# 118 spare 128x128 products on TensorE ahead of batch 0's steps, in a two-layer attention, expert and state-space kernel

## The chip, the cores and the metric

The kernel runs on one core of one Trainium2 chip. A core has TensorE (products and transposes, results into PSUM banks), VectorE, ScalarE and GpSimd for everything else, and queues that issue DMAs; SyncE's queue issues all of this kernel's. The engines run side by side, each through its own list of instructions in order, and wait for one another by semaphores. The metric is the time on the device of one execution, in microseconds, the median of several runs; lower is better.

## The reference

The input `x` is 4 batches of 512 rows of 128 features, with a context of 77 rows of 96 features for each batch. Four residual layers follow one another, each on a LayerNorm of `x`:

```python
x = x + L0_xattn(layernorm(x), ctx, ctx, ...)      # 16 heads of 8 features, 77 keys, softmax
x = x + L0_ffn(layernorm(x), ...)                  # 8 experts 128 -> 512 -> 128, the top 2 weighted
x = x + L1_xattn(layernorm(x), ctx, masks, ...)    # top-32 attention of 4 heads, FiLM, a state-space
                                                   # convolution by Fourier transform, a GELU MLP
x = x + L1_ffn(layernorm(x), rhs)                  # one product in int8 values with scales
```

All expert products are computed for all rows, in float32; the two picked experts get a weight and the others zero. The convolution's kernel is generated from its parameters inside the program (the `kgen` steps).

## The kernel before, in words

Everything is held on chip: rows on the 128 partitions, four tiles of 128 rows to a batch. The program is a list of 690 steps `(kind, batch, index)`. Five streams of steps, head and attention (H), experts (E), text attention (T), tail (O) and kernel generation (K), are merged into one list, `order`, by a string written out by hand (`ORDER`, line 138, read by `plan`). Each engine's block loops over that same list and does its part of each step, so the list sets the order of work on every engine. TensorE's block is the loop at line 632.

PSUM has eight banks here: two for the experts' first product (`moe_h`), two for their second (`moe_y`), four (`side`) that all other steps take in turn; a step's product waits until the former contents of its `side` bank were read. `moe_h[0]` is first written by the first expert product of batch 0.

Batch 0's steps up to the first expert product come in this order. A small setup of keys and values (lines 633 to 653). `norm_T` attn: four 128x128 transposes of the normalised input (line 629). `q_proj` (line 672), whose result ScalarE and VectorE split in three bf16 pieces that twelve DMAs spread over partitions (line 594). Four `setup_film` products (line 658), which wait for weights that GpSimd scales (line 1481), then `setup_rhs`. `smax`: 32 small bf16 products (line 681), whose row maxima VectorE takes (line 1100); `smax_T`: their transposes (line 629 again), which four DMAs spread (line 601). `kgen_base`: 43 short VectorE instructions (lines 1306 to 1348). Then the sixteen heads: `score` h (line 696, bf16, 50 rows by 77 columns of weights), an exponential on ScalarE (line 923), and `pv` h (line 706, float32, 77 by 72), one head behind. Two buffers `PT` take the exponentials.

Between scores 9 and 10 stands `kgen_tables` 0: VectorE's tables (lines 1360 to 1372), ScalarE's sines and exponentials (lines 980 to 988), GpSimd's products (lines 1516 to 1524). Behind them on ScalarE stands `attn_sum` 0 (line 927), which empties the bank of heads 0 to 7, after a reciprocal on VectorE (line 1110). `kgen_mm` 0 (line 852) stands before `pv` 15, and further tables before `attn_sum` 1. `attn_norm` (line 714), `o_proj` (line 721), LayerNorm, `norm_T` moe (line 629), `router` (line 727), the routing weights on VectorE (to line 1145), `w_T` (line 734), `b2_add` (line 741), and the first expert product `moe_up` (line 752). `moe_down` is line 764. Batch 1's head steps are then mixed with batch 0's experts.

A product of float32 operands leaves two MATMUL and two LDWEIGHTS records in the trace, a bf16 product or a transpose one each.

Of the kernel before, what the change touches and what calls it, by code (L numbers as in the profile page):

```python
# [14 lines left out]
P = 128  # L15
# [3 lines left out]
H0, HD0 = 16, 8  # L19
# [128 lines left out]
def needed(step, former):  # L148
# [10 lines left out]
    if kind == "score":  # L159
        return [("smax_T", b, 0)] + ([("pv", b, i - NPT)] if i >= NPT else [])  # L160
    if kind == "pv":
# [34 lines left out]
def plan():  # L196
# [9 lines left out]
    for run in ORDER.split():  # L206
        name = run[0]
        for _ in range(int(run[1:] or 1)):
# [11 lines left out]
         "score": 1, "attn_norm": 1, "o_proj": 1, "router": 1, "w_T": 1, "b2_add": 1, "text_q": 1, "topk": 1, "am_T": 1, "film": 1,  # L220
         "dft": 2, "idft": 1, "ffn_up": HC, "ffn_down": 1, "quant_T": 1, "quant_mm": 1, "kgen_mm": 1, "kgen_dft": 2}
SIDE = 4
NPT = 2


def place_fills(order):

    count, held, at, where = [0] * SIDE, set(), 0, {}

    def take(key):  # L230
        nonlocal at
        while at % SIDE in held:
            at += 1
        bank = at % SIDE
        where[key] = (bank, count[bank])
# [38 lines left out]
def recurrent_layers(nc, x, w1, w2, wpack, vpack, cpack, rpack, gpack, r2pack, xpack, dftf, dfti, b2, tmask, vmask, out):  # L274
# [10 lines left out]
    with ExitStack() as ctx:  # L285
        def sb(name, shape, dt=F32):
            return ctx.enter_context(nc.sbuf_tensor(name, shape, dt))

        def sem(name):
            return ctx.enter_context(nc.semaphore(name))  # L290
# [37 lines left out]
        def wc(name):  # L328
            return W[:, wcol[name][0]:wcol[name][1]]
# [16 lines left out]
        def xc(name):  # L346
            return XC[:, xcol[name][0]:xcol[name][1]]
# [29 lines left out]
        ZR = [m2.rearrange("p a s -> p (a s)").bitcast(F32), xnT["attn"]]  # L377
        PT = sb("PT", [NK, NPT, S])
        OV = qs
# [88 lines left out]
        moe_h = [ctx.enter_context(nc.psum_tensor(f"moe_h{i}", [P, 512], F32)) for i in range(2)]  # L468
        moe_y = [ctx.enter_context(nc.psum_tensor(f"moe_y{i}", [P, 512], F32)) for i in range(2)]
        side = [ctx.enter_context(nc.psum_tensor(f"side{i}", [P, 512], F32)) for i in range(SIDE)]  # L470


        side_full = [sem(f"side_full{i}") for i in range(SIDE)]
        side_read = [sem(f"side_read{i}") for i in range(SIDE)]
        x_in = [sem(f"x_in{b}") for b in range(B)]
# [39 lines left out]
        def free_for(pe, kind, b, i, n=0):  # L515

            k, m = FILL[(kind, b, i, n)]
            if m > 0:
                pe.wait_ge(side_read[k], m)
            return side[k], side_full[k]  # L520
# [7 lines left out]
        def emptied(eng, kind, b, i, n=0):  # L528

            k, m = FILL[(kind, b, i, n)]  # L530
            eng.wait_ge(side_read[k], m + 1)
# [14 lines left out]
        def pv_used(eng, b, h):  # L546

            if h % HG == HG - 1:
                k, m = FILL[("pv", b, 0, h // HG)]
                eng.wait_ge(side_full[k], m + 1)  # L550
            else:
                eng.wait_ge(pv_done, b * (H0 - 2) + h + 1 - h // HG)
# [70 lines left out]
        def _(pe):  # L623
# [6 lines left out]
                mm.then_inc(full, 1)  # L630

            for kind, b, i in order:
                if kind == "setup_k":
                    pe.wait_ge(xc_in, 16)
                    for n, w in enumerate(("wk", "wk1")):
                        dst, full = free_for(pe, kind, b, i, n)
                        pe.matmul(dst[:, 0:B * NK], xc(w), xc("ctxT"), start=True, stop=True).then_inc(full, 1)
                if kind == "setup_v":
                    dst, full = free_for(pe, kind, b, i, 0)
                    for b_ in range(B):  # L640
                        mm = pe.matmul(dst[0:NK, b_ * P:(b_ + 1) * P], xc("ctxT")[:, b_ * NK:(b_ + 1) * NK], xc("wv"),
                                       start=True, stop=True)
# [47 lines left out]
                if kind == "score":  # L690
                    dst, full = free_for(pe, kind, b, i)
                    if i == 0:
# [4 lines left out]
                              start=True, stop=True).then_inc(full, 1)  # L697
                if kind == "pv":

                    g, h = i // HG, i % HG  # L700
                    dst = side[FILL[("pv", b, 0, g)][0]]
                    if h == 0:
                        free_for(pe, "pv", b, 0, g)
                        pe.wait_ge(v_placed, b + 1)
                    emptied(pe, "score", b, i)
                    mm = pe.matmul(dst[0:GROWS, :], VP[:, g, GROWS * h:GROWS * (h + 1)], PT[:, i % NPT, :],  # L706
                                   start=(h == 0), stop=(h == HG - 1))
                    mm.then_inc(side_full[FILL[("pv", b, 0, g)][0]] if h == HG - 1 else pv_done, 1)
                if kind == "attn_norm":

                    dst, full = free_for(pe, kind, b, i)
                    for g in range(2):
                        pe.wait_ge(rz_ready, 2 * b + g + 1)
                        mm = pe.matmul(dst[64 * g:64 * g + 64, :], cc("spread")[64:GROWS, :], ZR[g][64:GROWS, :],
                                       start=True, stop=True)
# [7 lines left out]
                if kind == "router":  # L723
                    dst, full = free_for(pe, kind, b, i)
                    emptied(pe, "norm_T", b, "moe")
                    for t in range(T):
                        mm = pe.matmul(dst[:, t * E8:(t + 1) * E8], xnT_moe[:, b % 2, t * P:(t + 1) * P], wc("wr"),
                                       start=True, stop=True)
# [14 lines left out]
                if kind == "moe_up":  # L743
# [6 lines left out]
                    if n >= 2:  # L750
                        pe.wait_ge(moe_h_ready, n - 1)
                    pe.matmul(moe_h[n % 2][:], W1[:, e, c * P:(c + 1) * P], xnT_moe[:, b % 2, :],  # L752
                              start=True, stop=True).then_inc(moe_h_full, 1)
# [18 lines left out]
                if kind == "topk" and i[1] == 0:  # L772
                    t = i[0]
                    dst, full = free_for(pe, kind, b, t)
                    if t == 0:
# [5 lines left out]
                              start=False, stop=True).then_inc(full, 1)  # L781
# [26 lines left out]
                if kind == "idft":  # L808
# [3 lines left out]
                    for half in range(2):  # L812
                        for r in range(4):
                            y = (YR if r < 2 else YI)[:, r % 2, :, :]
                            mm = pe.matmul(dst[:, half * 2 * D:(half + 1) * 2 * D], FI[:, r, half * P:(half + 1) * P], y,  # L815
                                           start=(r == 0), stop=(r == 3))
# [40 lines left out]
        def _(act):  # L857
            for kind, b, i in order:
# [57 lines left out]
                if kind == "score":  # L916
                    src, read = filled(act, kind, b, i)
                    n = b * H0 + i
                    if i >= NPT:
                        pv_used(act, b, i - NPT)  # L920
                    elif b >= 1:
                        pv_used(act, b - 1, H0 - NPT + i)
                    act.activation(PT[:, i % NPT, :], src[0:NK, :], ACT.Exp).then_inc(read, 1)  # L923
# [674 lines left out]
```

## Time and profile before

| what | value |
|---|---|
| median of 3 runs | 673.56 us (670.68 to 678.76) |
| the profiled execution | 674.6 us, span 672.8 us |
| TensorE products busy | 526.3 us, 78% of the span, 2539 records |
| TensorE weight loads | 313.1 us, 47% |
| VectorE busy | 448.9 us, 67% |
| ScalarE, GpSimd busy | 239.6 us (36%), 136.6 us (20%) |
| mean granted TensorE clock | 0.844 |
| chain that ended last | TensorE 65%, VectorE 15%, issue 5% |

How to read it: the span is from the first to the last instruction of one profiled execution, and the device time includes a little around it. A busy share is an average over stages with different limits. The granted clock is the share of 2.4 GHz that TensorE is given: it is either 0.5 (1.2 GHz) or 1 (2.4 GHz), and a figure in between is a mean over a stretch.

### The profile page before, as it was taken

To read this page: it belongs to the slowest core of one execution; us is meant where nothing else is said; L and a number is where in the kernel's file an instruction comes from. 1 tells how busy PE (TensorE), PEld (TensorE's weight loads), DVE (VectorE), ACT (ScalarE), POOL (GpSimd) and SP (SyncE) were. 2 spreads that over 40 slices of the span, in tenths; PEclk is the share of its full clock that TensorE was granted. 3 is DMA by queue.
4 is the path that set the end of the run, shared out by engine and by line. 5 is a ranking of instruction groups with operands and counts; after the bars stand their busy time and mean duration, and the time that the engine had idled before them with its cause. 6 is when DMAs were issued, how large, how long until landed. Compare 5 with 4: busy or idle time off the path is not lost.

```text
span 672.8 us, 8058 instructions
## 1 busy us (share of the span) xinstructions
PE 526.3 (78%) x2539; PEld 313.1 (47%) x2539; DVE 448.9 (67%) x1770; ACT 239.6 (36%) x406; POOL 136.6 (20%) x164
## 2 busy tenths in 40 slices
PE   3449694297999999999999799999999974725360
PEld 2111133155644766644677665367657753403230
DVE  6279263638142458867577699678889978895616
ACT  3332541445434344344344264434354420411020
POOL 3501417232300020000142011015101151121211
PEclk8655555578999999999999899999999996755675
DMA  4519000003000003000002000000000000000000
GB/s 127 117 57 305 0 0 1 0 11 38 3 0 1 0 1 48 3 0 1 0 2 40 7 3 1 0 1 16 1 2 1 0 17 0 2 0 16 0 0 16
DMA packets 16156, 14.18 MB, mean 21 GB/s; under 512 B 1290, under 2 KB 14354, under 8 KB 16114
## 3 DMA queue, kind: packets, MB, share of 16 engines
q1 hardware_dynamic: 16114, 13.68, 8.5%
q8 instruction: 20, 0.33, 0.2%
q14 instruction: 22, 0.18, 0.1%
HBM read 8.86 MB, written 1.05 MB: 15 GB/s over the span
## 4 chain that ended last, share of the span: by engine, by line
PE 65%; DVE 15%; issue 5%; ACT 4%; SPq 4%; DMA 4%; POOL 2%; POOLq 0%; DVEq 0%
PE moe_y L764 15%; PE moe_h L752 15%; PE side L706 11%; SPq L594 4%; DMA QA<-Q 4%; PE side L696 4%; PE side L804 3%; PE side L815 2%; PE side L823 2%; PE side L792 2%; PE side L831 2%; DVE area L1184 2%; PE side L629 1%; PE side L852 1%; DVE TOP L1174 1%
## 5 line engine op out<-in xcount | busy, mean ns | idle before, releaser
L764 PEld LDWEIGHTS moe_y<-W,HT 128*128 128x128 f32 x1024 | 131.8, 194 | 45.6 <-issue 42.9
L764 PE MATMUL moe_y<-W,HT 128*128 128x128 f32 x1024 | 136.4, 279 | 0.0
L752 PE MATMUL moe_h<-xnT_moe,W 128*128 128x512 f32 x256 | 133.0, 608 | 0.0
L941 ACT ACTIVATE HT<-moe_h,W 128x512 f32<-128x512 f32 x128 | 87.6, 686 | 125.2 <-PE moe_h L752 124.7
L706 PE MATMUL side<-PT,VP 77*72 77x512 f32 x128 | 82.5, 735 | 0.7 <-ACT PT L923 0.7
L923 ACT ACTIVATE PT<-side 77x512 f32<-77x512 f32 x64 | 37.5, 591 | 59.6 <-PE side L696 59.5
L1160 DVE SCALAR_TENSOR_TENSOR X<-moe_y,RW,X 128x128 f32<-128x128 f32 x128 | 35.9, 343 | 25.1 <-PE moe_y L764 24.9
L752 PEld LDWEIGHTS moe_h<-xnT_moe,W 128*128 128x128 f32 x256 | 41.0, 195 | 13.0 <-issue 8.3
L1445 POOL TENSOR_TENSOR area<-area 128x128 f32<-128x128 f32 x16 | 7.3, 455 | 178.9 <-ACT area L958 178.9
L1184 DVE MATCH_REPLACE8 area<-TOP,area 128x77 f32<-128x77 f32 x192 | 40.6, 222 | 0.0
L696 PEld LDWEIGHTS side<-QA,KA 50*77 50x77 bf16 x64 | 7.1, 116 | 66.8 <-issue 59.0
L1100 DVE TENSOR_REDUCE mx<-side 128x6 f32<-128x462 f32 (+1 forms) x48 | 24.6, 577 | 20.1 <-PE side L681 20.1
L696 PE MATMUL side<-QA,KA 50*77 50x512 bf16 x64 | 28.4, 465 | 11.9 <-issue 6.3
L815 PE MATMUL side<-area,FI 128*128 128x256 f32 x64 | 19.2, 466 | 15.7 <-DVE area L1243 14.3
L1174 DVE MAX8 TOP<-area 128x8 f32<-128x77 f32 x192 | 31.2, 224 | 0.1
L681 PE MATMUL side<-KM,QA 128*128 128x154 bf16 x128 | 15.2, 266 | 13.7 <-DMA QA<-Q 13.3
L1110 DVE RECIPROCAL xT_head<-side 8x512 f32<-8x512 f32 x4 | 13.4, 3355 | 18.6 <-PE side L706 18.6
L792 PE MATMUL side<-FF,AMT 78*128 78x512 f32 x32 | 19.8, 705 | 6.9 <-ACT AMT L952 6.4
L706 PEld LDWEIGHTS side<-PT,VP 77*72 77x72 f32 x128 | 15.5, 160 | 20.1 <-issue 18.3
L815 PEld LDWEIGHTS side<-area,FI 128*128 128x128 f32 x64 | 15.0, 240 | 19.3 <-issue 16.4
L949 ACT ACTIVATE area<-area 128x308 f32<-128x308 f32 x16 | 7.4, 460 | 45.5 <-DVE area L1177 45.4
L785 PE MATMUL side<-C,AM 128*78 128x128 f32 x16 | 4.9, 307 | 22.1 <-DVE AM L1213 22.1
(306 smaller groups left out, 846.6 us busy)
## 6 DMA issues: line engine op xcount, KB each, us to landing
W<-in_w SPq DMA_DIRECT2D x8, 512.0 KB, 7.4
QA<-Q SPq DMA_DIRECT2D x48, 64.0 KB
X<-in_x SPq DMA_DIRECT2D x4, 256.0 KB, 6.2
out_dram<-FO SPq DMA_DIRECT2D x4, 256.0 KB, 2.3
V<-in_vpack SPq DMA_DIRECT2D x1, 579.0 KB, 3.5
area<-in_r2pack SPq DMA_DIRECT2D x1, 576.0 KB, 7.1
area<-in_gpack SPq DMA_DIRECT2D x1, 576.0 KB, 4.5
FW<-in_dftf SPq DMA_DIRECT2D x1, 512.0 KB, 7.5
```

Of the source, the lines that this page charges most:

```text
L594: sp.dma_start(QA[r0:r0 + HD0, :, :], Q3[64 * u:64 * u + 64, piece, :]).then_inc(q_spread, 16)
L696: pe.matmul(dst[0:NK, :], KA[r0:r0 + SROWS, i // 2, b * NK:(b + 1) * NK], QA[r0:r0 + SROWS, i // 2, :], start=True, stop=True).then_inc(fu ...
L706: mm = pe.matmul(dst[0:GROWS, :], VP[:, g, GROWS * h:GROWS * (h + 1)], PT[:, i % NPT, :], start=(h == 0), stop=(h == HG - 1))
L752: pe.matmul(moe_h[n % 2][:], W1[:, e, c * P:(c + 1) * P], xnT_moe[:, b % 2, :], start=True, stop=True).then_inc(moe_h_full, 1)
L764: mm = pe.matmul(moe_y[m % 2][:, t * P:(t + 1) * P], HT[:, m % 2, c, t * P:(t + 1) * P], W2[:, e, c, :], start=(c == 0), stop=(c == HC - 1))
L792: pe.matmul(dst[:], AMT[:, i % 2, :], FF[:, b, :], start=True, stop=True).then_inc(full, 1)
L815: mm = pe.matmul(dst[:, half * 2 * D:(half + 1) * 2 * D], FI[:, r, half * P:(half + 1) * P], y, start=(r == 0), stop=(r == 3))
L923: act.activation(PT[:, i % NPT, :], src[0:NK, :], ACT.Exp).then_inc(read, 1)
L941: act.activation(HT[:, m % 2, c, :], moe_h[n % 2][:], ACT.Relu, bias=wc("b1")[:, e * HC + c:e * HC + c + 1]).then_inc(moe_h_ready, 1)
L1160: ins = dve.scalar_tensor_tensor(X[:, b, t, :], moe_y[m % 2][:, t * P:(t + 1) * P], RW[:, b % 2, t, e:e + 1], X[:, b, t, :], ALU.mult, ALU ...
L1174: dve.max(TOP[:, a, h, r, :], s).then_inc(top_max, 1)
L1184: dve.match_replace(TW[:, h, :], TOP[:, a, h, r, :], s, PICKED)\
```

## The change

`SPARE` gives, for steps of batch 0, a number of spare products. TensorE issues them ahead of the step's own waits and work. Each multiplies two 128x128 blocks of weights that are in SBUF by then (`wq` and `wo`) into the first 128 columns of `moe_h[0]`, and nobody reads the result. They carry no wait and no signal. Counted by the list of steps there are 118: 16 + 12 + 8 + 6 + 12 + 4 + 3 + 20 + 4 + 16 + 3, and one for each of scores 2 to 15.

```diff
+SPARE = {("norm_T", "attn"): 16, ("setup_film", 0): 12, ("smax", 0): 8, ("smax_T", 0): 6, ("score", 0): 12,
+         ("attn_norm", 0): 4, ("o_proj", 0): 3, ("norm_T", "moe"): 20, ("router", 0): 4, ("w_T", 0): 16, ("b2_add", 0): 3,
+         **{("score", h): 1 for h in range(2, H0)}}
 NPT = 2
@@
             for kind, b, i in order:
+                for _ in range(SPARE.get((kind, i), 0) if b == 0 else 0):
+                    pe.matmul(moe_h[0][:, 0:P], wc("wq"), wc("wo"), start=True, stop=True)
                 if kind == "setup_k":
```

## Rows read from the trace of the kernel before

**Rows 1.** The page: busy tenths in 40 slices, TensorE and its granted clock.
```profile
PE   3449694297999999999999799999999974725360
PEclk8655555578999999999999899999999996755675
```
**Rows 2.** Stages: start:end, length, busy us (records) by engine, granted clock, DMA share, GB/s.
```profile
29.00:35.70 6.70, 3.00 (x20) 1.44 (x19) 0.81 (x2) 2.10 (x5) 1.65 (x6) 1.00 0.36 42
...
47.60:69.70 22.10, 21.32 (x27) 4.10 (x28) 19.08 (x37) 5.91 (x11) 3.29 (x2) 0.50 0.85 273
...
187.00:195.00 8.00, 8.00 (x19) 1.87 (x18) 2.15 (x5) 3.55 (x6) 0.00 (x0) 1.00 0.00 0
```
**Rows 3.** TensorE in order of time, to score 0: start, length, instruction [idle before].
```profile
15.87 1.09 PE L629 MATMUL side<-C,xn_head 128*128 128x128 f32 x4 [4.53 <-DVE xn_head L1077]
17.73 2.04 PE L672 MATMUL side<-xT_head,W 128*128 128x512 f32 x2 [0.78 <-ACT xT_head L897]
25.54 5.25 PE L658 MATMUL side<-area,VT 128*77 128x512 f32 x8 [5.77 <-POOL area L1481]
...
34.48 0.92 PE L681 MATMUL side<-KM,QA 128*128 128x154 bf16 x11 [3.51 <-DMA QA<-Q]
...
41.04 1.01 PE L629 MATMUL side<-C,mx 128*16 128x128 f32 x4 [1.51 <-DVE mx L1100]
47.63 0.65 PE L696 MATMUL side<-QA,KA 50*77 50x512 bf16 x2 [5.58 <-issue]
```
**Rows 4.** The same, heads of batch 0: a head, the next one's score, score 10.
```profile
50.91 0.65 PE L696 MATMUL side<-QA,KA 50*77 50x512 bf16 x1
51.48 1.98 PE L706 MATMUL side<-PT,VP 77*72 77x512 f32 x2
53.39 0.65 PE L696 MATMUL side<-QA,KA 50*77 50x512 bf16 x1
...
76.41 0.65 PE L696 MATMUL side<-QA,KA 50*77 50x512 bf16 x1 [5.54 <-ACT qs L927]
```
**Rows 5.** The same, two scores of batch 1.
```profile
188.41 0.41 PE L696 MATMUL side<-QA,KA 50*77 50x512 bf16 x1
...
189.76 0.41 PE L696 MATMUL side<-QA,KA 50*77 50x512 bf16 x1
```
**Rows 6.** The same, four 128x128 products cold and warm, warm steps, a short idle.
```profile
143.50 1.12 PE L764 MATMUL moe_y<-W,HT 128*128 128x128 f32 x8
144.46 0.60 PE L629 MATMUL side<-C,xn_head 128*128 128x128 f32 x4
145.84 1.10 PE L672 MATMUL side<-xT_head,W 128*128 128x512 f32 x2 [0.78 <-ACT xT_head L897]
...
162.69 2.00 PE L764 MATMUL moe_y<-W,HT 128*128 128x128 f32 x8
164.48 1.19 PE L681 MATMUL side<-KM,QA 128*128 128x154 bf16 x9
...
266.79 0.72 PE L681 MATMUL side<-KM,QA 128*128 128x154 bf16 x8 [1.60 <-DMA QA<-Q]
```
**Rows 7.** In order of time: table inputs on VectorE and ScalarE, then TensorE's late steps.
```profile
65.65 1.23 DVE L1372 TENSOR_TENSOR area<-area 128x1024 f32<-128x1024 f32 x1
...
71.95 1.04 ACT L984 ACTIVATE area<-area 128x1024 f32<-128x1024 f32 x1
...
75.79 0.57 ACT L927 ACTIVATE qs<-side 64x512 f32<-64x512 f32 x1
...
118.33 1.09 PE L629 MATMUL side<-C,xn_head 128*128 128x128 f32 x4 [4.89 <-DVE xn_head L1077]
...
126.28 1.06 ACT L984 ACTIVATE area<-area 128x1024 f32<-128x1024 f32 x1 [3.41 <-DVE area L1372]
...
132.75 1.01 PE L734 MATMUL side<-C,RW 128*8 128x128 f32 x4 [10.70 <-DVE RW L1145]
134.48 2.04 PE L741 MATMUL side<-B,xT_head 8*128 8x128 f32 x8 [0.72 <-issue]
```

## The prediction

> **What bounds the kernel now.** I read the page's slices first, then stages, then TensorE's own order in time. The slices [rows 1] are 16.8 us each: TensorE is above 90% from the twelfth slice to the thirty-third, so a microsecond lost or won before the first expert product stays in the end time nearly whole. The same rows show a granted clock of 0.5 in slices three to eight, about 34 to 135 us, which is exactly batch 0's attention. The stages [rows 2] say something less obvious: from 47.60 to 69.70 us TensorE is busy 21.32 of 22.10 us, and the clock is still 0.50 (the 1.2 GHz level) throughout. The same work in batch 1, 187 to 195 us, runs at 1.00 (2.4 GHz), with TensorE just as full. So this loop does not wake the clock by itself, but doesn't lose it once it has it. Its products are narrow: 50 of 128 rows for a score, 77 rows by 72 columns for a value product [rows 4]. What stood ahead of the rise at 29 us were the film products, 128 rows by 77 columns [rows 2, 3].
>
> Price of the low clock: one head (score start to score start) takes 53.39 - 50.91 = 2.48 us cold [rows 4] and 189.76 - 188.41 = 1.35 us warm [rows 5].
>
> The order of time [rows 3] gives the holes in front of TensorE's steps: 4.53 us before the first transposes, 5.77 before film, 3.51 before the maxima's scores, 1.51 before the maxima's transposes, 5.58 before score 0, and 5.54 before score 10 [rows 4]. The clock's memory shows too: after 3.51 us of idle at a high clock (30.97 to 34.48) the heads' stretch is cold [rows 2, 3], while after 1.60 us of idle up to 266.79 [rows 6] it was not lost: the slice around it, the sixteenth, has a granted clock of 9 tenths or more [rows 1].
>
> **The change, part by part.** It removes nothing, moves nothing, adds no wait and no DMA. It adds 118 products, 236 matmul records (a float32 product leaves two), each between two 128x128 operands. Their price: four such products from 162.69 to the next start at 164.48, so 1.79 / 4 = 0.45 us cold; from 143.50 to 144.46, so 0.96 / 4 = 0.24 us warm [rows 6]. They wait for nothing, so each starts as soon as the product ahead is through, and what matters is whether it ends before the step behind it was due.
>
> 1. Sixteen before the first transposes. TensorE is free at 15.87 - 4.53 = 11.34, the step starts at 15.87 [rows 3]. All warm: 3.8 us, hidden. All cold: 7.2 us, 2.7 late. I take half each, 5.5 us, 1.0 late, and then the transposes at 0.60 in place of 1.09 and the query product at 1.10 in place of 2.04 [rows 3, 6], which gives 1.4 back. Term -0.4, ends -1.4 and +2.7. The query's DMAs follow, so this moves everything behind it.
> 2. Twelve before film, eight before the maxima's scores: 5.4 and 3.6 us cold against 5.77 and 3.51 of idle. Hidden: term 0, end +0.1. Without that idle they'd cost 9.0 us.
> 3. Six before the maxima's transposes: cold 2.7 against 1.51, 1.2 late; warm 1.4, hidden, and the transposes (1.01) win 0.4. Term +0.3, ends -0.4 and +1.2.
> 4. Twelve before score 0, over the DMAs that spread the maxima. Warm 2.9, cold 5.4, against 5.58: hidden either way. But warm, they end 2.7 us before score 0 is due, and then come two short scores and a wait for the first exponential before products follow closely. That is nearer to the 3.51 us that lost the clock than to the 1.60 that did not. I take it that the heads begin with about one of them warm and are cold from then on: term -0.5, ends -0.9 and 0.
> 5. One before each of scores 2 to 15. In the cold loop TensorE is the bound; there is no hole to put a product in. The one before score 10 falls into the 5.54 us wait. Thirteen are left: 13 x 0.45 = **+5.85**. ScalarE's exponentials, tables and the sums wait for these products and come later by the same. Does one wide product per head wake the clock? Cold, it is 0.45 of 2.93 us; five sixths of TensorE's time remain the work at which the clock stayed down for 21 busy microseconds. I say no, and this is my least certain step. Ends: 0 and +5.85 for the products themselves; a woken clock is a rival below.
> 6. Four and three around the output projection lie beside a reciprocal and work that ends ahead of what the next LayerNorm needs. Twenty before its transposes (hole 4.89 [rows 7]): warm 4.8, mixed 6 to 7, cold 9.0. Lateness up to 3.41 us is covered, since ScalarE waits that long for VectorE's tables at 126.28 [rows 7]. Term 0, end +1 all cold. Four before the router and sixteen before the weights' transposes: 9.0 cold against 10.70 [rows 7], 0, end +1. Three before the bias product: 1.35 cold in 134.48 - 133.76 = 0.72 [rows 7]: +0.6, end 0.
> 7. The first expert's products begin cold as before: term 0. If the spares have the clock up by then, some 5 us from 136.5 on are halved [rows 1]: end -2.5.
>
> Sum: -0.4 + 0.3 - 0.5 + 5.85 + 0.6 = +5.85 us. The profiled execution took 674.6 us around its span of 672.8, so 680.5 for it; the median of the three runs, 673.56, lies 1.0 lower, so **679.4**.
>
> The Trainium skill (TensorE: Matmul & The Clock Gate, Part 1, "What's actually happening") says that the throttled state is the default and that a recently busy engine is given the full clock. By that rule the heads would be warm already, and the spares ahead of score 0 would make sure of it. The trace doesn't agree in this place: 21.32 us busy of 22.10 at 0.50 [rows 2]. What the rule would give is the second rival's time.
>
> **The rivals.** *First, half won:* the clock holds over the hole before score 0 and through heads 0 to 9, and is lost in the wait before score 10. The first half is then not TensorE's: ScalarE's tables sit in its queue between exponentials 9 and 10, and they need VectorE's last table, which ends at 66.88 [rows 7]. From that input to the attention sum, ScalarE took 75.79 - 71.95 = 3.84 us, so the sum can start at 70.7 in place of 75.79: -5.1. Five cold spares behind that cost +2.25, the bias product +0.6, the start -0.1: -2.3, 671.2 us. For it: the loop held 1.00 in batch 1. Against: the hole ahead of it.
>
> *Second, faster:* the spare in each head, or the burst ahead, wakes the clock for nearly the whole loop in both halves. Then the first half wins 5.1 as above, and heads 10 to 15 take 1.35 + 0.24 = 1.59 in place of 2.48, 6 x 0.89 = 5.3. With two microseconds of step 7: -12.4 in all, **661**. It decides at one place: whether a spare per cold head is enough. For it: wide products did precede the rises at 29 and at 141 us, and the rule named above speaks for it. Against: spares are a sixth of the loop's time.
>
> *Third, nothing:* between the score's start at 50.91 and the next one, the value product itself is 1.98 us of 2.48; if a spare fits into what is left (0.50 us, weight loads and starts), it costs nothing cold either, and the sum is about 673.5. Against: most of what is left is the score itself.
>
> **How the numbers follow.** Forecast 0.60 (its bounds add to 674 to 686); half won 0.09; faster 0.25; nothing 0.06. A measurement of this kernel tells about 1%, 6.7 us, from no change (three runs of it lie 8 us apart). The forecast's +5.85 lies just inside that; with the ends of steps 1, 3 and 6 I give 0.23 of its 0.60 to slower, 0.37 to within. Half won and nothing are within: 0.15. The faster case is all beyond 1%. So 0.25, 0.52, 0.23. The range must reach to the faster case, half of whose results lie above 661, and to 685 above: about 0.8 in it.
>
> **What would show it.** Granted clock between 48 and 70 us and the head period there: 0.5 and 2.9 us for the forecast, 1.00 and about 1.6 for both rivals with a gain, which part at the stretch from 71 to 90. Step 1: start of the transposes near 17 and of the maxima's scores near 34. Step 5: value products of 1.98 us with a spare behind each. Step 6: no wait on TensorE of VectorE or ScalarE before the router. The forecast is wrong if the clock rises anywhere inside the heads: from that point on each head gives back 0.9 us.

## The result, and the profile after

Twenty runs of the changed kernel have a median of 680.45 us (675.11 to 685.75), against 676.38 us (670.68 to 680.14) for the kernel before in as many runs; the ratio is 1.0061, with a 95% interval of 1.0036 to 1.0085. The forecast was 679.4 us. Four of the changed kernel's twenty runs, at 685.4 to 685.8 us, fell in a slower state of the chip, and the ratio is taken without them. The profiled execution took 680.76 us, its span 678.9, so 6.2 us more than the profiled one of before; the two medians lie 4.1 us apart.

Below, *cold* means a granted clock of 0.50 and *warm* one of 1.00, and a *burst* is several spare products in a row.

The page's slices of the kernel after, 17.0 us each, answer to [rows 1]: TensorE is fuller in the first three slices and in the seventh and eighth, and the granted clock from the fourth to the seventh is as low as it was.

```profile
PE   6679697777999999999999898999999973825360
PEclk8785555869999999999999899999999997665675
```

Stages of the kernel after (start:end and length, busy us and records of PE, PEld, DVE, ACT and POOL, granted clock, DMA share, GB/s), to be held against [rows 2]:

```profile
14.70:21.40 6.70, 5.92 (x47) 5.17 (x45) 1.72 (x5) 2.31 (x4) 0.32 (x1) 1.00 0.59 196
42.00:45.30 3.30, 3.08 (x28) 2.85 (x25) 2.01 (x7) 2.04 (x4) 0.00 (x0) 1.00 0.02 5
45.40:48.70 3.30, 0.41 (x2) 0.14 (x2) 2.99 (x10) 2.34 (x5) 0.00 (x0) 1.00 0.29 60
48.80:74.80 26.00, 25.67 (x44) 9.98 (x44) 20.33 (x34) 7.08 (x12) 3.29 (x2) 0.50 0.68 225
```

The first line runs from the warm part of the first burst over the transposes and the query product to the twelve spares behind it; TensorE is busy 5.92 of 6.70 us there. The second and third lines are the idle time (the hole) before score 0. The twelve spares fill its first half warm; in the second half TensorE works 0.41 of 3.30 us, and the line behind it, the heads, is at 0.50 throughout, though TensorE is busy 25.67 of 26.00 us.

TensorE of the kernel after in order of time (start, length, instruction, idle before it), against [rows 3, 4, 7]; line 637 is the spare product. The last line is of the kernel before:

```profile
16.38 0.60 PE L632 MATMUL side<-C,xn_head 128*128 128x128 f32 x4
17.76 1.10 PE L677 MATMUL side<-xT_head,W 128*128 128x512 f32 x2 [0.78 <-ACT xT_head L902]
...
25.90 6.50 PE L663 MATMUL side<-area,VT 128*77 128x512 f32 x8 [4.37 <-POOL area L1486]
...
34.19 0.91 PE L686 MATMUL side<-KM,QA 128*128 128x154 bf16 x11
...
41.66 0.73 PE L632 MATMUL side<-C,mx 128*16 128x128 f32 x4
...
47.98 0.41 PE L701 MATMUL side<-QA,KA 50*77 50x512 bf16 x2 [2.90 <-issue]
...
51.44 0.65 PE L701 MATMUL side<-QA,KA 50*77 50x512 bf16 x1
52.01 1.98 PE L711 MATMUL side<-PT,VP 77*72 77x512 f32 x2
53.78 0.63 PE L637 MATMUL moe_h<-W 128*128 128x128 f32 x2
54.35 0.65 PE L701 MATMUL side<-QA,KA 50*77 50x512 bf16 x1
...
79.93 0.64 PE L701 MATMUL side<-QA,KA 50*77 50x512 bf16 x1 [5.12 <-ACT qs L932]
...
96.98 3.60 PE L857 MATMUL side<-area 128*32 128x16 f32 x64
...
125.87 0.60 PE L632 MATMUL side<-C,xn_head 128*128 128x128 f32 x4
...
138.41 1.01 PE L739 MATMUL side<-C,RW 128*8 128x128 f32 x4 [6.46 <-DVE RW L1150]
...
142.64 7.26 PE L757 MATMUL moe_h<-xnT_moe,W 128*128 128x512 f32 x10
149.73 1.12 PE L769 MATMUL moe_y<-W,HT 128*128 128x128 f32 x8
...
136.45 3.78 PE L752 MATMUL moe_h<-xnT_moe,W 128*128 128x512 f32 x4
```

The head period is 54.35 - 51.44 = 2.91 us, where it was 2.48 [rows 4]. Score 0 is 0.35 us late, score 10 is 3.52 late, the first expert product (136.45 before, 142.64 now) 6.2 late, the first down product 149.73 - 143.50 = 6.2 [rows 6], and so is the end of the span, 6.1.

In the experiments below, "the first expert product" is the start of the first line with `moe_h<-xnT_moe`. It is the sharper measure: it sums all that happened in the stretch under study, while the whole time also has what the clock does later. In the run without the heads' spares, for instance, the first expert product came 0.3 us late and the profiled span was 5.1 us longer; its median of twelve runs is that of the kernel before.

One trace stands for each kernel, and the traces differ also where the kernels do not. Score 0 is at 47.63 us in the kernel before, and at 47.31 to 48.09 in the five runs below whose kernels hold no spare ahead of it. In the seven traces that have the change's own spares up to the maxima's transposes, these transposes start anywhere from 40.45 to 42.38 us. So a difference of less than about a microsecond in the first expert product is not told apart from that spread.

### The profile page after: what moved, and what is told of

It reads as the page before. It is cut to its first block, busy times and chain, and to the rows that moved or that the text cites. A ratio compares the mean times of both kernels' runs of the same rounds, so it can differ in the third digit from the quotient of the medians.

```text
span 678.9 us, 8530 instructions
## 1 busy us (share of the span) xinstructions
PE 559.5 (82%) x2775; PEld 351.5 (52%) x2775; DVE 448.9 (66%) x1770; ACT 239.7 (35%) x406; POOL 137.0 (20%) x164
## 4 chain that ended last, share of the span: by engine, by line
PE 67%; DVE 16%; ACT 4%; issue 4%; SPq 4%; DMA 3%; POOL 2%; POOLq 0%; DVEq 0%; ACTq 0%
PE moe_y L769 15%; PE moe_h L757 14%; PE side L711 11%; PE side L701 4%; PE side L809 3%; SPq L597 3%; DMA QA<-Q 3%; PE side L828 2%; PE side L820 2%; PE moe_h L637 2%; PE side L797 2%; PE side L836 2%; DVE area L1189 2%; PE side L857 1%; DVE TOP L1179 1%
## 5 line engine op out<-in xcount | busy, mean ns | idle before, releaser
L637 PEld LDWEIGHTS moe_h<-W 128*128 128x128 f32 x236 | 41.0, 251 | 19.1 <-issue 19.0
L637 PE MATMUL moe_h<-W 128*128 128x128 f32 x236 | 41.7, 337 | 0.0
L1115 DVE RECIPROCAL M<-side 8x512 f32<-8x512 f32 x4 | 13.4, 3356 | 15.2 <-PE side L711 9.5
```

Of the source, the lines that this page charges most:

```text
L637: pe.matmul(moe_h[0][:, 0:P], wc("wq"), wc("wo"), start=True, stop=True)
```

## The experiments

**Which spares cost.** Two kernels divide the change: the heads' spares alone, and all the others alone.

Each diff below shows what differs, with `...` for the rest of a line. These two are against the changed kernel.

```diff
-SPARE = {("norm_T", "attn"): 16, ... , **{("score", h): 1 for h in range(2, H0)}}
+SPARE = {("score", h): 1 for h in range(2, H0)}
```

> Only the fourteen spares ahead of scores 2 to 15; all bursts between steps are gone. Theory (the spares in the cold heads are the whole loss): head period 2.91 us and granted clock 0.50 from 48 to 69 us, 13 x 0.43 = +5.6 us on the first expert product against the kernel before, ratio about 1.008, and about the time of the changed kernel. Rival (the bursts made it slower, for instance by the late maxima's transposes and the late bias product): about +1 us here, ratio 1.00.

Measured: 680.38 us, ratio 1.0083 (1.0051 to 1.0115); first expert product at 141.78 us, 5.3 us late.

```diff
          ... ("w_T", 0): 16, ("b2_add", 0): 3,
-         **{("score", h): 1 for h in range(2, H0)}}
+         }
```

> The changed kernel without the fourteen spares ahead of scores 2 to 15: 104 spares in bursts between steps. Theory: heads at 2.49 us each and cold again after the first; what is left is +0.3 us at score 0, -0.3 for the warm first scores, +0.5 at the bias product, so the first expert product at +0.5 us against the kernel before, ratio 1.000 to 1.002. Rival (the bursts cost as much as the heads' spares): +3 us or more.

Measured: 673.58 us, ratio 0.9987 (0.9962 to 1.0012); first expert product at 136.72 us, 0.3 us late. The fourteen single products by themselves give the changed kernel's time (680.45 us); the 104 others cost and bring nothing that can be measured.

**Would more wide products in each head wake the clock?**

Against the kernel before, which has no spares:

```diff
+SPARE = {("score", h): 3 for h in range(2, H0)}
```

> Three spares ahead of each of scores 2 to 15 in place of one, no bursts. Theory (one wide product per head was too little against the narrow products around it): with 1.3 us of wide products in 3.8 us the clock rises within the first heads; from there a head takes 1.35 + 3 x 0.22 = 2.0 us, under the 2.49 of the kernel before: first half ahead by 2 to 3 us, second half by 0 to 2, in all -2 to -5 us, ratio 0.993 to 0.997. Rival (spares inside the heads never wake it, whatever their number): 39 x 0.43 = +17 us, ratio 1.025.

Measured: 690.68 us, ratio 1.0224 (1.0190 to 1.0259); first expert product at 153.37 us, 16.9 us late, for 39 x 0.43 = 16.8 of spares. The rival was right and my theory was wrong. Stages of this run, the heads of each half:

```profile
51.00:81.00 30.00, 30.00 (x73) 15.83 (x72) 18.30 (x29) 5.65 (x9) 3.29 (x2) 0.50 0.51 166
87.00:108.20 21.20, 21.20 (x48) 10.25 (x48) 7.80 (x11) 3.57 (x6) 6.51 (x5) 0.50 0.00 1
```

TensorE is busy for 30.00 of 30.00 us at 0.50, a third of it (3 x 0.43 of the 3.77 us of a head) with products that fill all 128 rows.

**Where is the clock lost?** From here on the heads hold no single spares. First the hole before score 0 is filled to its end. Against the kernel without the heads' spares:

```diff
-... ("smax_T", 0): 6, ("score", 0): 12, ...
+... ("smax_T", 0): 6, ("score", 0): 24, ...
```

> As the run without the heads' spares, but 24 products in place of 12 ahead of score 0, so that the 5.6 us hole there is full at the warm price of 0.22 us each. Theory (the clock was lost in the 2.9 us of idle that were left and the sparse start of the heads; the heads hold a warm clock by themselves): granted clock 1.00 from 48 us on, head period 1.35 us without any spare, exponential 9 near 61 us; then VectorE's table at 67 us bounds the first half, the attention sum starts at 70.7 to 71.2 in place of 75.8, and the second half is cold: -4 to -5 us on the first expert product, ratio 0.993. Rival (batch 0's heads can't hold the clock, which batch 1 held only because expert products stand around them): the clock is down again within two heads and the time is within 1 us of the kernel before.

Measured: 671.54 us, ratio 0.9962 (0.9932 to 0.9992); first expert product at 134.23 us, 2.2 us early. Between the theory and the rival. Stages of this run: the hole, the first three microseconds of the heads, the rest of the first half; then the wait inside the second of them, on TensorE.

```profile
41.00:46.60 5.60, 5.49 (x50) 5.30 (x48) 4.36 (x13) 4.18 (x7) 0.00 (x0) 1.00 0.05 10
46.70:49.60 2.90, 2.16 (x6) 0.63 (x7) 2.63 (x9) 1.40 (x3) 0.00 (x0) 1.00 1.03 317
49.70:66.00 16.30, 16.30 (x21) 2.85 (x19) 15.13 (x29) 3.73 (x7) 3.29 (x2) 0.50 0.96 311
...
47.85 1.05 PE L711 MATMUL side<-PT,VP 77*72 77x512 f32 x2 [0.74 <-ACT PT L928]
```

The hole is full and the heads begin warm; the second line is where it goes wrong: 2.16 us busy of 2.90. Its idle part is the 0.74 us in which the first value product waits for the first exponential. So three more products were put there, ahead of score 1. Against the kernel above:

```diff
-... ("score", 0): 24, ...
+... ("score", 0): 24, ... ("score", 1): 3}
```

> As the run with 24 products ahead of score 0, and three more ahead of score 1, in the 0.74 us in which TensorE waits for the first exponential; no other spares in the heads. In that run the clock was 1.00 when the heads began and fell 3 us later, over the sparse first microsecond. Theory: with that wait filled the heads keep 1.00 at 1.35 us each, exponential 9 ends near 61 us, ScalarE waits for VectorE's last table (65.7 to 66.9 us), the attention sum starts at 69.8 to 70.7 against 75.8 before, score 10 to 15 are cold again: first expert product 5 to 6 us earlier than before, ratio 0.992. Rival (batch 0's heads lose the clock whatever precedes them): period back at 2.49 us by head 3, and the 2.5 us of the former run again, ratio 0.996.

Measured: 670.24 us, ratio 0.9920 (0.9888 to 0.9952); first expert product at 130.93 us, 5.5 us early. Stages of this run, the first half and the second:

```profile
46.60:60.00 13.40, 13.36 (x34) 3.68 (x34) 12.24 (x29) 6.29 (x11) 3.29 (x2) 1.00 1.05 341
...
70.40:85.20 14.80, 14.80 (x18) 2.69 (x18) 7.54 (x11) 3.55 (x6) 6.56 (x5) 0.50 0.00 1
```

Heads 2 to 9 of batch 0 hold the clock without a single spare among them, once they have it. Whether it was the three products or only the idle time gone that kept it up in the first microsecond, no run tells apart. What bounds the first half is then VectorE's table. ScalarE of this run (the same columns as TensorE's rows), at its first sine, at the wait, and at the attention sum; then score 10 on TensorE:

```profile
60.92 0.63 ACT L985 ACTIVATE area<-area 128x512 f32<-128x512 f32 x1
...
65.90 1.06 ACT L989 ACTIVATE area<-area 128x1024 f32<-128x1024 f32 x1 [3.41 <-DVE area L1377]
...
69.75 0.57 ACT L932 ACTIVATE qs<-side 64x512 f32<-64x512 f32 x1
```

```profile
70.38 0.65 PE L701 MATMUL side<-QA,KA 50*77 50x512 bf16 x1 [10.39 <-ACT qs L932]
```

From the input of line 989 to the sum it is 69.75 - 65.90 = 3.85 us, the 3.84 of the prediction's first rival. TensorE ends its nine value products 10.39 us before score 10 can start, and behind that wait it is cold. The next run fills it; against the kernel above:

```diff
-... ("score", 1): 3}
+... ("score", 1): 3, ("score", 10): 42}
```

> As the run before it, and 42 products ahead of score 10, to fill the wait for ScalarE's tables and the attention sum (about 9.8 us at 0.22 us each). Theory: the clock stays 1.00 from 31 us to the end of the heads, the second half takes 1.35 us a head too, kernel generation's first products (line 857 there) start near 79 us and take 2.2 in place of 3.6; VectorE's second tables bound what follows: first expert product 11 to 13 us earlier than before, ratio 0.981 to 0.984. Rival (if the clock is lost before score 10, the 42 products cost 0.43 us each): 42 x 0.43 = 18 us against a wait of 5.5 to 10, so +5 to +12 us, ratio 1.01 to 1.02.

Measured: 668.04 us, ratio 0.9866 (0.9816 to 0.9916); first expert product at 131.75 us, 4.7 us early. The gain of 11 us did not come. Stages of this run: the 42 products, the first microseconds of the second half, and its rest:

```profile
62.30:71.80 9.50, 9.50 (x85) 9.31 (x83) 9.08 (x9) 5.78 (x7) 0.00 (x0) 1.00 0.50 161
72.80:74.60 1.80, 1.80 (x5) 0.54 (x6) 0.00 (x0) 0.61 (x2) 1.70 (x2) 1.00 0.00 0
74.80:86.00 11.20, 11.20 (x14) 1.81 (x12) 5.98 (x10) 2.74 (x5) 4.72 (x3) 0.50 0.01 2
```

After 0.97 us of idle at 71.8 the second half began warm and lost the clock two microseconds on. Its score 0 also stood at 49.04 us, 2.4 later than in the run before, though both kernels are the same up to there. The clock came up at other places in this execution: the first transposes were already 1.3 us later (17.56 for 16.26), the burst ahead of the maxima's transposes began 1.1 later and took 2.85 us in place of 1.54, and these transposes were cold (1.06 for 0.60). VectorE's tables follow the maxima: ScalarE's line 989 got its input at 68.30 in place of 65.90 us, so the first half, which they bound, ended 2.4 us later too.

**Wide, or only busy?** Two runs replace wide spares by narrow ones: the same instructions and columns, with 32 of 128 rows.

The first is the kernel with 24 and 3 products; only its bursts ahead of scores 0 and 1 are narrow.

```diff
+                    k = 32 if kind == "score" else P
-                    pe.matmul(moe_h[0][:, 0:P], wc("wq"), wc("wo"), start=True, stop=True)
+                    pe.matmul(moe_h[0][:, 0:P], wc("wq")[0:k], wc("wo")[0:k], start=True, stop=True)
```

> As the run that holds the first half, but the products ahead of scores 0 and 1 use 32 of the 128 rows of both operands: as many instructions, columns and microseconds of TensorE busy, a quarter of the array's rows. Theory (narrow products don't count in full toward the clock): the clock is lost within the burst ahead of score 0, the products take 0.43 us each from there, score 0 comes up to 5 us late, and the heads are cold at 2.49 us. Rival (only TensorE's busy time counts): as the run that holds the first half, head period 1.35 us.

Measured in one run: 679.16 us. Stages of this run: the narrow burst ahead of score 0, first and second part, then heads. The last two lines are the burst ahead of score 0, here and with wide products in the run with 42.

```profile
43.10:47.00 3.90, 3.90 (x33) 3.87 (x33) 2.80 (x10) 2.90 (x7) 0.00 (x0) 0.93 0.02 6
47.10:50.50 3.40, 3.40 (x17) 3.22 (x16) 3.10 (x9) 1.17 (x1) 0.00 (x0) 0.50 0.57 173
50.60:73.00 22.40, 22.40 (x33) 5.18 (x32) 16.46 (x31) 5.33 (x9) 3.29 (x2) 0.50 0.75 243
...
43.13 7.49 PE L638 MATMUL moe_h<-W 32*128 32x128 f32 x48
...
43.23 5.88 PE L637 MATMUL moe_h<-W 128*128 128x128 f32 x48
```

The clock rose half a microsecond into the burst, behind the wide products before it, and was lost inside it with TensorE busy all the time; the products behind took nearly twice as long (17 records in 3.40 us against 33 in 3.90). Score 0 came at 50.55 us, against 46.63 in the run with 24 and 3 wide products; but 1.7 of these 3.9 us stood already at the maxima's transposes (42.14 against 40.45), where the two kernels are alike. The fair comparison is the run with 42: there too the burst began cold, at 43.23 us, but with wide products the clock rose and stayed, and it took 5.88 us for the 7.49 here. The loss is 1.6 us, and the heads behind it are cold in the one and warm in the other.

**Together in place of singly.** The kernel before with two bursts of ten wide products, one in each half, and nothing else.

```diff
+SPARE = {("score", 2): 10, ("score", 11): 10}
```

> The kernel before with ten products ahead of score 2 and ten ahead of score 11 and no others: 20 spares, in place of the 14 single ones, concentrated so that no narrow product stands between them. Theory (wide products wake the clock when they stand together, and the heads then keep it): each burst takes 3.5 to 4.3 us, the clock is 1.00 by its end, heads 2 to 9 take 1.35 us and end near 66 us, so VectorE's table bounds the first half (attention sum at 70.7 against 75.8); the second half ends 2 to 3 us ahead on top of that: first expert product 7 to 9 us earlier, ratio 0.987 to 0.990. Rival (the heads never keep the clock in batch 0): 20 x 0.43 = +8.6 us, ratio 1.013.

Measured: 668.93 us, ratio 0.9899 (0.9851 to 0.9947); first expert product at 127.90 us, 8.6 us early. TensorE of this run in order of time, the first burst and two heads behind it:

```profile
50.98 3.20 PE L635 MATMUL moe_h<-W 128*128 128x128 f32 x20
54.11 0.41 PE L699 MATMUL side<-QA,KA 50*77 50x512 bf16 x1
54.45 1.08 PE L709 MATMUL side<-PT,VP 77*72 77x512 f32 x2
55.45 0.41 PE L699 MATMUL side<-QA,KA 50*77 50x512 bf16 x1
```

Ten products take 3.1 us and the period is 1.34 us from there to the end of the first half. The same with 32 rows, against this kernel:

```diff
-                    pe.matmul(moe_h[0][:, 0:P], wc("wq"), wc("wo"), start=True, stop=True)
+                    pe.matmul(moe_h[0][:, 0:P], wc("wq")[0:32], wc("wo")[0:32], start=True, stop=True)
```

> The two bursts of ten ahead of scores 2 and 11, with 32 of the 128 rows of both operands: the same instructions and columns, a quarter of the rows. Theory (width is what counts): the clock stays 0.50, each burst takes 10 x 0.43 = 4.3 us, the heads 2.49 us each, first expert product 8.6 us later than in the kernel before. Rival (an unbroken run of any products wakes it): as with the wide bursts, heads at 1.35 us from score 2 on and the first expert product 8.6 us earlier.

Measured in one run: 684.07 us. TensorE of this run at the same place, and the first expert product, 8.8 us late; the granted clock is 0.50 from 50 to 100 us, so neither of its two bursts raised it:

```profile
50.58 4.63 PE L635 MATMUL moe_h<-W 32*128 32x128 f32 x20
55.15 0.64 PE L699 MATMUL side<-QA,KA 50*77 50x512 bf16 x1
...
57.63 0.65 PE L699 MATMUL side<-QA,KA 50*77 50x512 bf16 x1
...
145.24 3.78 PE L755 MATMUL moe_h<-xnT_moe,W 128*128 128x512 f32 x4
```

**The change with its spares placed together.** Against the changed kernel:

```diff
-         **{("score", h): 1 for h in range(2, H0)}}
+         ("score", 2): 10, ("score", 11): 10}
```

> The changed kernel with its fourteen single products in the heads replaced by ten ahead of score 2 and ten ahead of score 11; all its other bursts as they are. It has more spares in the heads than the change, and differs from it only in how they stand. Theory (it was the placing, one wide product between narrow ones, that lost): first expert product 7 to 9 us earlier than in the kernel before and 13 to 15 us earlier than in the changed one, ratio 0.987 to 0.990. Rival (the change's other bursts spoil what the two bursts win): less than 3 us earlier, ratio over 0.995.

Measured: 665.72 us, ratio 0.9878 (0.9834 to 0.9922); first expert product at 130.63 us, 5.8 us early, and 12.0 earlier than in the changed kernel. Both bursts took 4.4 us here against 3.1 and 3.6 in the run with bursts alone: they were at 0.50 from end to end, and the clock came up only behind them (the score after the first took 0.57 us, in between 0.65 and 0.41). The whole time is that of the theory, the stretch falls 1.0 to 1.2 us short of it.

So ten is no safe number. In the changed kernel the twenty spares ahead of the LayerNorm's transposes stood at 0.50 for their first 4.80 us, about eleven products:

```profile
119.00:123.80 4.80, 4.80 (x24) 4.78 (x23) 3.64 (x6) 1.06 (x4) 3.98 (x3) 0.50 0.00 0
```

**The experts' start.** The last two kernels also fill the 10.7 us wait before the routing weights' transposes, and differ in how the first half gets its clock.

```diff
+SPARE = {("score", 2): 10, ("score", 11): 10, ("w_T", 0): 36, ("b2_add", 0): 3}
```

> The kernel with two bursts of ten in the heads, and 36 products ahead of the routing weights' transposes, over the 10.7 us in which TensorE waits for them, with three more ahead of the bias product. Theory: the 36 are cold for about 3.5 to 6 us and then warm, 9.5 to 11 us in all, so the transposes are on time within 1 us; the transposes take 0.60 in place of 1.01, the bias product about 1.1 in place of 2.0, the spares ahead of it fit into its 0.72 us wait, and the ten records of the expert products no longer start cold: expert stage's first down product 3 to 4.5 us earlier than in the run with the two bursts alone, ratio to the kernel before 0.983 to 0.986. Rival (the sparse bias product and its waits lose the clock again): within 1 us of the run with the two bursts.

Measured: 663.70 us, ratio 0.9844 (0.9809 to 0.9879). TensorE of this run in order of time, from the 36 products to the first down product:

```profile
113.63 10.25 PE L635 MATMUL moe_h<-W 128*128 128x128 f32 x72
124.48 0.60 PE L737 MATMUL side<-C,RW 128*8 128x128 f32 x4 [0.60 <-DVE RW L1148]
124.91 0.83 PE L635 MATMUL moe_h<-W 128*128 128x128 f32 x6
125.80 1.12 PE L744 MATMUL side<-B,xT_head 8*128 8x128 f32 x8
126.85 4.93 PE L755 MATMUL moe_h<-xnT_moe,W 128*128 128x512 f32 x10
131.62 1.12 PE L767 MATMUL moe_y<-W,HT 128*128 128x128 f32 x8
```

The first down product is 2.6 us earlier than with the two bursts alone (134.26) and 11.9 earlier than before; the expected 3 to 4.5 us were a little too much. The bursts stood 0.3 us later in this run, and the expert products win 1.4 us (4.93 for 6.35), where step 7 of the prediction had at most 2.5.

```diff
+SPARE = {("score", 0): 20, ("score", 1): 3, ("score", 11): 10, ("w_T", 0): 36, ("b2_add", 0): 3}
```

> Twenty products ahead of score 0 and three ahead of score 1 in place of the ten ahead of score 2, then ten ahead of score 11, and the 36 and 3 before the experts; nothing earlier. Theory: the twenty start cold and warm on the way, 5 to 7 us in a 5.6 us wait, so score 0 is up to 1.5 us late, but all ten heads of the first half are warm; VectorE's table bounds them in any case, so the first half is at best 0.3 us ahead of the run with the burst ahead of score 2, and the whole within 1 us of it, ratio 0.983 to 0.988. Rival (the first half's bound is TensorE): 3 us ahead of it.

Measured: 662.61 us, ratio 0.9833 (0.9790 to 0.9877); score 10 at 71.57 us and the first expert product at 126.62, 0.2 us from the run above in both. TensorE was through with the first half 3.4 us earlier than in the run above and won nothing by it: ScalarE waited 3.22 us for VectorE's table there, as the theory has it. These two are the fastest kernels of the study, 1.6% under the kernel before; between the two no difference is shown.

## Why the prediction was right, step by step

The direction and the mechanism were right, and the size nearly: 5.85 us were summed, 6.2 us stand between the profiled executions, and 4.1 us between the medians of twenty. That the absolute forecast, 679.4 us, came within 1.1 of 680.45 is partly luck. It was built on a median of three runs, 673.56; the kernel before has 676.38 in the twenty runs beside the changed kernel's, and 5.85 us on top of that would have been 682.2 (in the rounds of the experiments it has 674.55 to 674.94). The main term is as it was priced. The small ones of steps 1 to 3 came to -0.9, +0.6 and +0.6 and nearly cancelled in this trace. In the seven traces with the same spares up to the maxima's transposes these start at 40.45 to 42.38 us, against 41.04 before, so the sum of these terms is anything from -0.6 to +1.3 us, and one trace can't confirm it. By its steps, in the profiled execution:

1. Sixteen spares at the start, -0.4: the transposes were 0.5 us late and warm, the query product warm, and what ScalarE makes of it came at 18.89 in place of 19.81 us, -0.9.
2. Film and maxima, called hidden: wrong by +0.6. The film products were cold for longer (0.50 up to 31 us, 0.66 from 31 to 32; in the kernel before 1.00 from 29 us on), 6.50 in place of 5.25 us, and the eight spares behind them ended only at 34.2. So the scores of the maxima began 0.3 early and not 0.9. The spares account for some 0.2 of that: in the run with 24 products these scores waited for their DMAs alone and began at 33.97.
3. The maxima's transposes, +0.3: they began 0.6 us late, ran partly warm, and were 0.3 late at their end; against step 2's -0.3 that is +0.6.
4. The hole before score 0, -0.5: measured -0.3. Score 0 is 0.35 us late and score 10 is 3.52, so 3.17 us were added between them, by eight spares of 0.43, 3.44 us; the rest is the warm beginning. The clock went where step 4 put it, behind the first scores.
5. One in each head, +5.85: measured +5.6, thirteen times 0.43; I had taken 0.45 from four products with an uneven last start. This is the term that decided, and the run with the heads' spares alone shows it by itself (+5.3). The least certain link, that one wide product doesn't wake the clock, held, and so did three.
6. The later bursts, 0: the LayerNorm's transposes were 7.5 us late against 5.65 ahead of them and behind them, and nothing waited: ScalarE still waits 2.37 us for VectorE's table at 131.94. The bias product took +0.5, forecast +0.6.
7. The experts' cold start stayed, as forecast; the run with 36 products shows what it was worth, 1.4 us on the expert products and 2.6 in all.

One reading of the rows was loose and changes no term: TensorE is not above 90% in every slice from the twelfth to the thirty-third, but at 7 tenths in the twenty-third and the thirty-third [rows 1].

Two of the rivals were borne out where their condition, a warm clock in the heads, was made to hold. *Half won* is the run with 24 and 3 products: attention sum 3.85 us behind line 989's input, the first half 6 us shorter, the clock lost in the wait before score 10. *Faster* was decided at another place than I wrote: not by whether a spare per head is enough, but by whether the wide products stand together. Its 12.4 us were nearly reached by the last two kernels, 10.9 and 11.9 us under the median of the kernel before in the same round. *Nothing*, a spare hidden in the head's 0.50 us, is refuted by the period of 2.91 us.

The Trainium skill (TensorE: Matmul & The Clock Gate, "Why this matters for your kernels") advises to keep TensorE continuously busy for the full clock. That rule the runs here don't bear out as it stands: 30.00 us busy of 30.00 at 0.50, and a clock lost within a burst of 32-row products. With 128-row products in a row the clock did come up, behind ten of them in each of the four runs that had such bursts, though in one of the four only once the burst was over, and elsewhere after more of them.

Left open: the narrow spares changed the rows only, so what fewer columns would do was not tried, and each of the two kernels with narrow spares was run once. Nor is it shown why a burst raised the clock after 1.6 us in one run and after more than 4.4 in another.

## What to carry to other kernels

This is what one kernel showed, to be tried anew in another. A full TensorE row at a granted clock of 0.50 is a stretch that runs at half speed; look at the shapes of its products before adding work to it. Spare products paid where they stood together, filled 128 rows, and lay in a wait or at the head of a loop that then kept the clock by itself; a spare in every iteration of a loop that TensorE bounds cost its full length, and neither one nor three of them raised the clock. Price them cold, give a burst more than ten, follow the clock to the next wait, a fraction of a microsecond at the start of a loop included, and read which other engine bounds the stretch once TensorE is fast.

## What the runs showed of the hardware

- The same loop is stable at either clock: 2.49 us a head at 0.50 for more than 20 us, 1.34 us a head at 1.00, with TensorE all but full in both.
- Three 128-row products among the narrow ones of each head left the clock at 0.50 for 30 us; ten in a row, in records of 3.20 to 4.47 us, raised it in seven bursts of seven, for two of them only once they were over; ten of 32 rows did not, in two bursts of one execution. Twenty of 128 rows stood at 0.50 for their first 4.80 us at another place.
- A full, warm burst was followed by a lost clock when the stretch behind it was busy for 2.16 of 2.90 us with narrow products; with three wide products in that place (0.94 us in the trace) it was kept, in each of three runs.
- Behind a fast TensorE, VectorE's table is the next bound: ScalarE waited 3.2 to 3.4 us for it in the three runs that were warm from score 0 on, none at all in the three with a burst ahead of score 2, where in two it started line 987 just as the table was through and in one a microsecond later. With the first half warm, score 10 started at 70.38 us in the run that began its scores at 46.63, at 71.48 to 71.79 in three of the runs with a burst of ten, and at 72.78 and 72.89 in the two whose scores or burst came later, against 76.41 in the kernel before; TensorE waited 0.97 us ahead of score 10 behind 42 spares and up to 10.39 without.
